# A fused two-layer network: first pair's queries and keys placed on chip, a shorter first lead of maxima, mixing's first rows fetched in the experts' stage

## The reference, cut to what matters

```python
q = heads(hidden_states @ Wq.T + bq)      # k and v alike; 64 blocks of 64 tokens
# blocks 2 to 61 see the first block, their own and two neighbours, and the last block
band = jnp.concatenate([first_band, inner, last_band], axis=-1)
aw = jax.nn.softmax(band, axis=-1)
# blocks 0 and 63 see all keys; blocks 1 and 62 see four blocks
...
moe = jnp.einsum('td,te->td', y, cw); out = shared + moe
...
kv = (k * v).transpose(1, 0, 2)           # state = ew * state + kv over the tokens
x = x + mixer_scale * (r * wkv @ Wo.T)
```

## Time and profile before

| what | us |
|---|---|
| median of 3 runs | 1872.55 (1872.14 to 1872.62) |
| the profiled execution's own time | 1870.89 |
| its span | 1869.1 |
| busy, of the span: PE / VectorE / ScalarE / POOL | 1634.1 / 1173.2 / 919.1 / 607.0 |

### The profile page before, as it was taken

The page is one execution under the profiler, slowest core; times in us unless marked ns, Lnnn a source line. Parts: engine busy times, 40 slices in busy tenths (PEclk is TensorE's granted clock), DMA queues, the critical chain, the costliest instruction groups (busy, mean ns, idle before and its releaser), DMA issues. The chain is left out here.

```text
span 1869.1 us, 35581 instructions
## 1 busy us (share of the span) xinstructions
PE 1634.1 (87%) x12958; PEld 1368.3 (73%) x12958; DVE 1173.2 (63%) x2482; ACT 919.1 (49%) x2016; POOL 607.0 (32%) x561
## 2 busy tenths in 40 slices
PE   8879999999994688899999498899983699999991
PEld 6777777777773478588888254589982699999991
DVE  7767667777666676555555488666657455555543
ACT  4217787777784443533333365544430344444434
POOL 3420000000042554677775154233320322222121
PEclk9989999999996899999999699999995699999996
DMA  8891434432315601244443621001114223333315
GB/s 287 289 144 46 64 71 82 82 62 63 55 47 192 237 34 46 53 72 74 72 71 48 155 57 42 1 24 46 46 53 151 43 80 95 88 96 83 83 16 180
DMA packets 143784, 164.90 MB, mean 88 GB/s; under 512 B 70794, under 2 KB 115968, under 8 KB 143616
## 3 DMA queue, kind: packets, MB, share of 16 engines
q1 hardware_dynamic: 107248, 111.47, 22.5%
q0 software_dynamic: 28544, 47.35, 12.0%
q10 hardware_dynamic: 7824, 3.81, 1.4%
HBM read 104.75 MB, written 61.08 MB: 89 GB/s over the span
## 5 line engine op out<-in xcount | busy, mean ns | idle before, releaser
L830 DVE TENSOR_REDUCE att_neg_max<-att_m_ps 128x1 f32<-128x320 f32 x496 | 216.9, 488 | 106.3 <-PE att_m_ps L550 103.9
L1929 PE MATMUL silu_h_ps<-silu_xT,silu_w_part 128*128 128x320 f32 x1536 | 236.4, 312 | 1.2 <-DVE silu_xT L2025 0.9
L1929 PEld LDWEIGHTS silu_h_ps<-silu_xT,silu_w_part 128*128 128x128 f32 x1536 | 227.0, 189 | 2.6 <-DVE silu_xT L2025 1.3
L550 PE MATMUL att_m_ps<-att_k,att_q 96*128 96x384 f32 x496 | 183.5, 384 | 8.1 <-DMA att_q<-qk 6.1
L1894 POOL DMA_INDIRECT summed<-silu_y,all_table x40 | 63.6, 1590 | 256.1 <-DVE silu_y L2065 149.6
L948 POOL DMA_DIRECT2D att_q<-att_max_row x40 | 20.2, 506 | 380.9 <-DVE att_max_row L838 379.0
L1655 POOL DMA_INDIRECT part<-layer_xT,all_table x72 | 118.7, 1648 | 59.9 <-DVE layer_xT L1776 50.2
L550 PEld LDWEIGHTS att_m_ps<-att_k,att_q 96*128 96x128 f32 x496 | 95.0, 191 | 38.7 <-issue 18.1
L1941 PE MATMUL silu_y_ps<-silu_w_part,silu_h_part 128*128 128x256 f32 x960 | 116.5, 283 | 2.2 <-DVE silu_w_part L2041 2.2
L1941 PEld LDWEIGHTS silu_y_ps<-silu_w_part,silu_h_part 128*128 128x128 f32 x960 | 115.9, 192 | 2.5 <-DVE silu_w_part L2041 2.5
L1684 PE MATMUL gelu_h_ps<-gelu_wu_part,gelu_xT 128*128 x402 | 110.1, 409 | 2.7 <-DVE gelu_wu_part L1783 2.5
(11 more groups left out here) (315 smaller groups left out, 4002.3 us busy)
## 6 DMA issues: line engine op xcount, KB each, us to landing
experts_w<-in_dram SPq DMA_DIRECT2D x24, 1024.0 KB
qk<-qkv_part POOLq DMA_DIRECT2D x32, 512.0 KB, 4.8
att_k<-qk SPq DMA_DIRECT2D x192, 64.0 KB, 2.4
att_q<-qk SPq DMA_DIRECT2D x168, 64.0 KB, 4.0
v<-qkv_v POOLq DMA_DIRECT2D x8, 544.0 KB, 6.2
att_v<-v SPq DMA_DIRECT2D x8, 544.0 KB, 5.4
qkv_x<-in_dram SPq DMA_DIRECT2D x8, 512.0 KB, 4.9
rows<-att_context SPq DMA_DIRECT2D x8, 512.0 KB, 5.4
```

The costliest lines, as they stand in the source:

```text
L550: nc.tensor.matmul(bank[:, 0:2 * LOCAL].rearrange("p (a n) -> p a n", a=2), q[b][0:MROW, x, :], local_and_global(b, x), start=True, stop=T ...
L830: ins = nc.vector.tensor_reduce(neg_max[b][:, x - 1:x], bank[:, 0:LOCAL + 2 * BLK], AX.X, ALU.max, negate=True)
L1929: mm = nc.tensor.matmul(h_ps[u % 2][a][:, :], w12_part[f % RING][wp][:, a, k, :], xT[s][xp][:, k, rows], start=(i == 0), stop=(i == 3 * KD ...
```

## The change

The 16 feature rows of each piece that belong to the first pair of heads are no longer written to memory. SP copies them on chip from `part[j]` into `q0` and `k0`, tiles that are now allocated ahead of the projection and are `q[0]` and `k[0]` of attention: three copies per piece, of 16 partitions each, and for keys in the first and the last group three more for the global blocks. POOL clears `q0` and the strip of `k0` and fills its row of ones at the projection's start, and SP waits for that (`place_cleared`) ahead of input group 2; the load of input group `g + 2` now stands ahead of group `g`'s copies in SP's stream. VectorE waits for the copies of a piece (`placed`) as well as for its write before it overwrites it. At attention's start nothing is loaded for the first pair but its values, 8 products stand in place of 36, and two behind each of the maxima of the lead in place of one. The lead ahead of the first scores is 6 steps of maxima; steps 0 to 11 then do 18 steps of maxima in place of 12, and from step 12 on the order is as before. POOL clears the second pair's tiles only behind the first row of maxima. In the experts' stage SP and ScalarE, not POOL, wait for the last sums, and each then issues six transfers with the tokens of mixing's groups 0 and 1, into the second half of `x`. The decays are loaded and their exponentials taken in that stage, too. Mixing's ScalarE begins with a square root of one element, and the ring of three holds groups 2 and up.

```diff
-            for g in range(2, NGRP):
-                load_x(g)
+            sp.wait_ge(place_cleared, 4)
+            for g in range(NGRP):
+                if g + 2 < NGRP:
+                    load_x(g + 2)
+                for j in range(4):
+                    t, a = j // 2, j % 2
+                    sp.wait_ge(low_done, 4 * g + j + 1)
+                    for i, h in enumerate((0, 0, 1) if t == 0 else (0, 1, 0)):
+                        r = 48 * a + HD * i
+                        of = part[j][0:HD, h, :].bitcast(F32)
+                        if t == 0:
+                            sp.dma_start(q0[r:r + HD, GB * g:GB * (g + 1), a * BLK:(a + 1) * BLK].bitcast(F32),
+                                         of.rearrange("f (l t) -> f l t", t=BLK)).then_inc(placed[j], 16)
+                            continue
+                        sp.dma_start(k0[r:r + HD, g * GRP:(g + 1) * GRP].bitcast(F32), of).then_inc(placed[j], 16)
+                        if g in ENDS_OF:
+                            to = T if g == 0 else T + BLK
+                            sp.dma_start(k0[r:r + HD, to:to + BLK].bitcast(F32), of[:, ENDS_OF[g]:ENDS_OF[g] + BLK]
+                                         ).then_inc(placed[j], 16)
             finish_prefetch(sp)
+            for j in range(4):
+                sp.wait_ge(placed[j], 16 * places(NGRP - 1, j))
 
...
                         dve.wait_ge(part_out[j], 16 * i)
+                        dve.wait_ge(placed[j], 16 * places(i - 1, j))
                     nc.vector.tensor_copy(part[j][:, 0, :], whole[:, s, :]).then_inc(high_done, 1)
...
-            dst = qk_d.rearrange("t h (g p) n -> p t h g n", p=P)
+            own = slice(HD, P)
+            dst = qk_d.rearrange("t h (g p) n -> p t h g n", p=P)[own]
+            nc.gpsimd.memset(q0[0:3 * 2 * HD, 0:NBLK // 2, :].bitcast(U32), 0).then_inc(place_cleared, 1)
+            nc.gpsimd.memset(q0[0:3 * 2 * HD, NBLK // 2:NBLK, :].bitcast(U32), 0).then_inc(place_cleared, 1)
+            nc.gpsimd.memset(k0[0:3 * 2 * HD, T + 2 * BLK:T + 3 * BLK].bitcast(F32), 0.0).then_inc(place_cleared, 1)
+            nc.gpsimd.memset(k0[3 * 2 * HD:3 * 2 * HD + 1, :].bitcast(F32), 1.0).then_inc(place_cleared, 1)
             pool.wait_ge(ones_set, 1)
             for i in range(0, NGRP):
                 for j in range(4):
                     t, g = j // 2, j % 2
                     pool.wait_ge(low_done, 4 * i + j + 1)
-                    pool.dma_start(dst[:, t, :, g, bass.ds(i * GRP, GRP)], part[j][:, :, :].bitcast(F32)
+                    pool.dma_start(dst[:, t, :, g, bass.ds(i * GRP, GRP)], part[j][own, :, :].bitcast(F32)
                                    ).then_inc(part_out[j], 16)
                 pool.wait_ge(v_copied, GT * (i + 1))
                 pool.dma_start(v_d.rearrange("h p t v -> p h t v")[:, :, bass.ds(i * GT, GT), :],
...
     STEPS = FULL + DB
-    LEAD = 12
+    LEAD, FIRST_LEAD = 12, 6
...
 
+        def maxima_until(g):
+
+            return min(FIRST_LEAD + g + 1 + min((g + 1) // 2, LEAD - FIRST_LEAD), TOTAL)
+
         def maxima_of(g):
 
-            return divmod(g + LEAD, STEPS) if g + LEAD < TOTAL else None
+            return [(n // STEPS, n % STEPS, at) for n in range(maxima_until(g - 1), maxima_until(g))
+                    for at in range(len(M[n % STEPS]))]
...
 
-            load_globals(0)
-            for c in range(CHUNKS):
-                load_keys(0, c)
             load_values(0)
-            sp.wait_ge(kg_in, 96)
             load_globals(1)
             for c in range(CHUNKS):
-
-                sp.wait_ge(qk_in[c], 192)
                 load_keys(1, c)
-                sp.wait_ge(cleared[1], c + 1)
+                sp.wait_ge(cleared, c + 1)
                 load_queries(sp, 1, c)
...
 
-            idle_products(36)
-            pe.wait_ge(padded, 2)
-            pe.wait_ge(o_cleared, 1)
-            for n in range(LEAD):
+            idle_products(8)
+            for n in range(FIRST_LEAD):
                 for at in range(len(M[n])):
                     maxima(0, n, at)
-                    idle_products(1)
+                    idle_products(2)
+            pe.wait_ge(padded, 1)
+            pe.wait_ge(o_cleared, 1)
             for g in range(TOTAL):
                 ms = maxima_of(g)
-                units = len(M[ms[1]]) if ms is not None else 0
-                for at in range(max(units, 3)):
-                    if at < units:
-                        maxima(*ms, at)
+                for at in range(max(len(ms), 3)):
+                    if at < len(ms):
+                        maxima(*ms[at])
...
         def _(act):
-            for c in range(CHUNKS):
-                act.wait_ge(cleared[0], c + 1)
-                load_queries(act, 0, c)
             act.wait_ge(probs_cleared, 1)
...
         def _(dve):
-            for c in range(CHUNKS):
-                nc.vector.memset(q[0][:, c * CB:(c + 1) * CB, :].bitcast(U32), 0).then_inc(cleared[0], 1)
...
-            for b in range(2):
-                nc.gpsimd.memset(k[b][MROW:ROWS, :].bitcast(F32), 1.0).then_inc(ones_set, 1)
-            for c in range(CHUNKS):
-                nc.gpsimd.memset(q[1][0:MROW, c * CB:(c + 1) * CB, :].bitcast(U32), 0).then_inc(cleared[1], 1)
-            pool.wait_ge(ones_set, 2)
             nc.gpsimd.memset(prob_b[0][:, :, :, :], 0.0)
             nc.gpsimd.memset(prob_b[1][:, :, :, :], 0.0).then_inc(probs_cleared, 1)
             pool.wait_ge(vg_cleared, 1)
+            copy_globals(0)
+            lay_row(0, 0)
+            pool.wait_ge(globals_copied, COPIES)
+            nc.gpsimd.memset(k[1][0:MROW, T + 2 * BLK:T + LOCAL].bitcast(F32), 0.0).then_inc(padded, 1)
+            for c in range(CHUNKS):
+                nc.gpsimd.memset(q[1][0:MROW, c * CB:(c + 1) * CB, :].bitcast(U32), 0).then_inc(cleared, 1)
+            nc.gpsimd.memset(k[1][MROW:ROWS, :].bitcast(F32), 1.0).then_inc(ones_set, 1)
+            pool.wait_ge(ones_set, 1)
             for p in range(PAIRS):
-                copy_globals(p)
-                for h in range(PARTS):
+                if p > 0:
+                    copy_globals(p)
...
                                              compute_op=ALU.add).then_inc(y_out[n % YS], 16)
+        def all_added(eng):
             for i in range(YS):
-                pool.wait_ge(y_out[i], 16 * (NT // YS))
+                eng.wait_ge(y_out[i], 16 * (NT // YS))
+
+        @block.sync
+        def _(sp):
+            next_decays(sp)
+            all_added(sp)
+            next_tokens(sp, 0)
 
         @block.tensor
...
                 high_piece(n)
+            next_decays(act)
+            all_added(act)
+            next_tokens(act, 1)
 
...
+        ring = [[m.sb(f"{a}{i}", [P, GT, D]) for i in range(BS)] for a in ("base", "second")]
+        base, second = ([x[:, TT // 2 + GT * (2 * g + a):TT // 2 + GT * (2 * g + a + 1), :] for g in range(2)] +
+                        [ring[a][g % BS][:, :, :] for g in range(2, NGRP)] for a in range(2))
...
-                if g >= BS:
+                if g >= BS + 2:
...
-            load(0)
+                    for at, js, piece in token_pieces(part_d, a, g):
+                        sp.dma_start(half[g][at, js, :], piece).then_inc(base_in[g % BS], 16)
+
             for i, a in enumerate((WkT, WvT, WrT)):
                 sp.dma_start(w[:, i], a.rearrange("(k p) n -> p k n", p=P)).then_inc(w_in, 16)
-            load(1)
             sp.dma_start(wo[:, :, :], WoT.rearrange("(k p) n -> p k n", p=P)).then_inc(w_in, 16)
             sp.dma_start(scale_row[:, :], row(scale).broadcast_to([P, D])).then_inc(w_in, 16)
-            for k in range(KD):
-                for a, b in ((td, decay), (tf, first_share)):
-                    sp.dma_start(a[:, k:k + 1], b[k * P:(k + 1) * P].rearrange("(p a) -> p a", a=1)).then_inc(w_in, 16)
             for g in range(2, NGRP):
...
+            nc.scalar.activation(first[:, :], eps[:, 0:1], ACT.Sqrt)
             step(-2)
-            act.wait_ge(w_in, NW)
-            nc.scalar.activation(e1[:, :], td[:, :], ACT.Exp).then_inc(e1_done, 1)
-            nc.scalar.activation(eu[:, :], tf[:, :], ACT.Exp)
-            act.wait_ge(e1_done, 1)
-            nc.scalar.activation(ew[:, :], e1[:, :], ACT.Exp, scale=-1.0).then_inc(shares_done, 1)
...
+            def next_decays(eng):
+
+                if eng is nc.sync:
+                    for k in range(KD):
+                        for a, b in ((td, decay), (tf, first_share)):
+                            eng.dma_start(a[:, k:k + 1], b[k * P:(k + 1) * P].rearrange("(p a) -> p a", a=1)).then_inc(decays_in, 16)
+                    return
+                eng.wait_ge(decays_in, 32 * KD)
+                nc.scalar.activation(e1[:, :], td[:, :], ACT.Exp).then_inc(e1_done, 1)
+                nc.scalar.activation(eu[:, :], tf[:, :], ACT.Exp)
+                eng.wait_ge(e1_done, 1)
+                nc.scalar.activation(ew[:, :], e1[:, :], ACT.Exp, scale=-1.0).then_inc(shares_done, 1)
+
```

(7 more changed lines are left out.)

122 lines of the change are left out of this document (69 added, 53 removed).

## The result

The change makes the kernel slower. Its median is 1889.78 us (1887.94 to 1891.37) against 1872.35 us (1871.81 to 1872.62) for the kernel before on the same chip, a ratio of 1.0093 [1.0076, 1.0111]. The forecast was 1851.5 us.

A forecast was written before the change was run, and what follows sets the result against it. Tensor engine busy 87%, but transfers bound attention's start; the projection had little transfer time to spare. Projection and attention -15.7 us, mixing -5.3, together -21.0 against the 1872.55 us median: 1851.5 us, range 1846 to 1863.

The forecast's parts named there:

- Projection: Projection stage: SP's added copies fit the 8.8 us group period at 0.445 us each; the stage grows by 2.3 us.
- The third rival: Projection: SP cannot issue copies at 0.445 us, a group takes 12.4 us against 8.8, time 1877 us; chance 0.04.
- (a) the input behind the copies: Projection: input group 3's load stands behind group 0's 18 copies and lands late, +1 us (0 to 2).
- (b) the clears: Projection's start: SP and POOL wait for clears until about 11.5 us, at no cost (1 us if POOL's load is slow).
- (c) the end: Projection's end: the last two pieces' twelve copies compete with POOL's last write, +1.3 us (0 to 4).
- The writes "an eighth smaller": Projection: smaller writes to memory stand against the copies' costs, saving 0.6 us of transfer time per group.
- The first rival: Projection: copies make it transfer-bound, each group 1.5 to 2.9 us longer, time 1859 to 1869 us; chance 0.18.
- Lead: Attention's start: no first-pair loads and a lead of 21 units for 46; step 0 at 104.4 us, -24.6 us.
- Steps 0 to 11: Attention: 25 units moved out of the lead cost +5.6 us, POOL's clears and SP's query loads +1 us.
- Mixing: Mixing's start: early tokens and table load bring the first projection from 1055.20 to 1049.9 us, -5.3 us.
- Experts: Experts' stage: no separate term in the sum; its end moving 3.6 us for the six issues was counted at mixing's start.

The follow-up runs named there:

- q_flat: The changed kernel with query copies in 16 pieces of 2 KB in place of 128 of 256 B: 1887.16 us, ratio 1.0081.
- x_act: The changed kernel with ScalarE, not SP, issuing the loads of input groups 2 to 7: 1883.13 us, ratio 1.0073.
- clears_all_rows: The changed kernel without SP's copies of queries and keys, and with all 128 partitions written to memory: 1848.39 us, ratio 0.9869.
- all_rows: The changed kernel with queries and keys written to memory at all 128 partitions again: 1893.55 us, ratio 1.011.
- from_memory: The changed kernel writing all 128 partitions, ScalarE issuing inputs, SP reading the first pair back from memory two groups at a time: 1857.96 us, ratio 0.9923.
- mix_g0: The kernel before with only the mixing part, and only group 0's tokens fetched in the experts' stage: 1864.31 us, ratio 0.9961.
- values_late: The changed kernel with the eight writes of values issued behind all writes of queries and keys: 1892.03 us, ratio 1.0102.
- x_act_kpool: The changed kernel with ScalarE issuing inputs of groups 2 to 7 and POOL issuing the copies of keys: 1887.71 us, ratio 1.008.
- keys_act: The changed kernel with two buffers for each piece and the copies of keys on ScalarE's queue: 1898.69 us, ratio 1.0137.
- lead_only: The kernel before with only the short lead, all loads from memory, values loaded behind the first chunk of keys: 1882.77 us, ratio 1.0048.
- from_memory_32k: The kernel with the first pair read back from memory, now group by group (102 loads for 54), and only group 0's tokens fetched early: 1863.8 us, ratio 0.9949.

## Why the prediction was wrong, point by point

- **Projection, +2.3 us forecast, +37.4 measured.** This step failed, and nearly all of the error is here (35 of 38 us). The sum priced a copy at 0.445 us, from six loads that ran with nothing beside them. The copies cost 0.63 us alone and 0.96 us on average in the projection; by the prediction's own sum the change is a loss from about 0.94 us on. The row with the right conditions was in the same group, 24 loads in 23.86 us, 0.99 us each; I put its length down to its pieces and not to what ran beside it. `q_flat` shows that the pieces had little to do with it. The third rival, with 12.4 us a group, had both the mechanism and the period (12.55 us), and I gave it 0.04. Its time, 1877 us, is still 13 us short: of the 37.4 us the longer period is 29, a later first split 1.6 (14.3 us against 12.7) and the end 6.8, and the experts' stage adds 4.0. That 0.99 us from scattered loads met 0.96 us from copies is partly luck, for the two differ in kind and size. Why an issue grows beside traffic stays open (see the hardware).
- *(a) the input behind the copies, +1.* It cost 2 to 3 us (`x_act`). *(b) the clears, 0:* right within 1 us, `clears_all_rows` starts the next stage at 89.1 us against 88.2. *(c) the end, +1.3:* it took 6.8 us: SP still issues query copies when the last piece is ready at 112.3 us, and its last twelve from 113.81 to 123.88 us.
- *The writes "an eighth smaller"* were booked as a gain. They are the slower form: 10 us lost in the kernel without copies. In the changed kernel this loss is hidden behind SP's copies (`all_rows`). No term of the sum had that, nor a rival.
- *The first rival* (transfer-bound) is not what happened: the share fell, and `from_memory` moves the same bytes with the splits at the old pace (8.85 us a group). The Trainium skill, page DMA: Bandwidth & Descriptors, section Rules for kernel authors, says that transfers under 64 KB are mostly overhead. The runs agree in this sense: a 32 KB and a 4 KB copy both take 0.63 us of issue alone, and 64 KB loads moved the same bytes with half the issues, 8.6 us sooner. Its section Specifications asks for 512 B or more for the full rate; that decided little here: 2 KB in place of 256 B gave 4 us.
- **Lead, -24.6 forecast, -23.3 measured** (18.0 us from stage start to step 0, 16.2 forecast). The unit of a maximum with two filling products took 0.62 us in place of 0.59. No new wait came last.
- **Steps 0 to 11, +6.6 forecast (5.6 and 1), +8.5 measured.** The mechanism was right, the term 1.9 us too small; the second row of maxima was not waited for.
- **Mixing, -5.3 forecast, -7.1 measured.** The stage end was booked 3.6 us late for the six issues. It isn't: from the last sum to the next stage it takes 8.9 us, as it did before (9.0). The issues are not free, since with three a queue (`mix_g0`) it takes 7.75 us; what was saved against them is not shown (the wait for the sums moved from POOL to SP and ScalarE in the same edit). Against that, the tokens ended last at 1066.05 us, 2.2 us into the stage.
- **Experts, 0 forecast, +4.0 measured;** see below. With the measured terms in place, the sum is 37.4 - 23.3 + 8.5 + 4.0 - 7.1 = +19.5 us, the 19.6 measured.

## What to carry to other kernels

Count a queue's issues and price each by a row with the same traffic beside it; then ask who waits for the transfer, since an issue stream longer than the loop's period leaves the loop's pace alone when it only reads memory (though its length can still set the end of the stage), and becomes the loop's period when it holds a buffer that the loop must rewrite. Where a stage is full of transfers, leaving data out of a write is no gain by itself: its shape can cost more than its bytes. And the hand-over that the change was after was worth having: without copies step 0 would start 23 us sooner than before, and read back from memory, in few large loads, 14.6 of these 23 us remain (first scores at 114.9 us against 129.5).

## What the runs showed of the hardware

- SP's issue of one transfer took 0.465 us from memory (64, 32 or 8 KB) and 0.63 us on the chip (32 or 4 KB) when alone; beside the projection's traffic the averages were 1.02 us (32 KB from memory), 0.98 us (32 KB on the chip, 82 issues, four of them inputs, from 33.67 to 113.81 us of the changed kernel) and 1.21 us (64 KB from memory). What makes an issue longer is not shown; less traffic (`values_late`) did not shorten it much, and fewer copies beside a second queue of copies (`x_act_kpool`) made it longer. Nor is it shown that the issuing itself is the limit and not the service behind the queue: with the copies split over two queues (`x_act_kpool`, `keys_act`) SP paused for 26 and 58 us in all, and a group took 12.6 and 13.75 us.
- With writes of 112 partitions all transfers together moved 289 GB/s, with writes of 128 they moved 346, at the same share. Why is open.
- A transfer of 8 KB, the row of maxima, landed 12 us after its issue beside queued loads (`lead_only`).
- The experts' stage has two lengths, 279 and 283 us. In the first 31 us of the stage in the profiles of before and after, the granted clock was 0.89 and 0.78:

```profile
749.00:780.00 31.00, 23.70 (x93) 15.09 (x94) 13.47 (x15) 14.62 (x16) 20.06 (x14) 0.89 0.26 56
```

```profile
772.00:803.00 31.00, 24.45 (x84) 14.61 (x84) 12.96 (x15) 13.97 (x15) 18.11 (x14) 0.78 0.26 52
```

All 20 profiles go by this: ten with 0.89 in these 31 us took 279.0 to 279.5 us, nine with 0.78 took 282.8 to 283.5, and one with 0.83 (`from_memory_32k`) took 281.4. Kernels with the changed kernel's own code for this stage stand on both sides (`x_act` 279.0, `x_act_kpool` 283.4). So 4 of the 19.6 us may be no property of the change; what sets the clock there was not tried.
